# A spectral-layer kernel: its inverse stage in steps of two quarters, all products on 64x64 tiles

## The reference

```python
h = jnp.einsum('bhwi,ic->bhwc', x, fc0_w) + fc0_b          # 3 -> 64 channels
h = h.transpose(0, 3, 1, 2)
for l in range(LAYERS):                                     # 4
    sc = _spectral_conv(h, w1r[l] + 1j * w1i[l], w2r[l] + 1j * w2i[l])   # rfft2, 32x16 modes mixed, irfft2
    pw = jnp.einsum('bihw,oi->bohw', h, pw_w[l]) + pw_b[l][None, :, None, None]
    y = sc + pw
    mean = y.mean(axis=(0, 2, 3), keepdims=True)
    var = y.var(axis=(0, 2, 3), keepdims=True)
    y = (y - mean) * jax.lax.rsqrt(var + EPS)
    y = y * gamma[l][None, :, None, None] + beta[l][None, :, None, None]
    h = jax.nn.gelu(y, approximate=False)
```

## Time and profile before

| | us |
|---|---|
| median of 3 runs | 2692.91 (2688.74 to 2693.61) |
| profiled execution | 2692.11 |
| its span | 2690.3 |
| TensorE busy | 2267.7 (84%) |
| ScalarE busy | 1717.2 (64%) |
| VectorE busy | 1704.0 (63%) |
| bytes moved by DMA | 537.18 MB, mean 200 GB/s |

### The profile page before, as it was taken

One profiled execution on the slowest core, in us unless ns is written; L12 is line 12 of the kernel. 1 busy time (PEld: TensorE's weight loads), 2 busy tenths in 40 slices (PEclk: granted clock), 3 DMA queues, 4 the chain that ended last, 5 costly groups with the idle time before them and its releaser, 6 DMA issues. The chain is left out here.

```text
span 2690.3 us, 75014 instructions
## 1 busy us (share of the span) xinstructions
PE 2267.7 (84%) x32251; PEld 1466.2 (54%) x32251; DVE 1704.0 (63%) x2585; ACT 1717.2 (64%) x2771; POOL 191.9 (7%) x237
## 2 busy tenths in 40 slices
PE   7679989966997997699899859996993777765999
PEld 4556657754664776566567656662221666642444
DVE  4767878884776887577778757771005776634443
ACT  2823358875776887667678766777992777721333
POOL 0000000000000000000000000000002222202443
PEclk9889989998998999899999989998996899976999
DMA  5746577558997774799977379996541000012332
GB/s 173 237 144 219 213 275 258 192 191 277 360 347 281 279 248 153 247 350 361 335 266 259 124 249 328 366 341 233 179 140 35 1 1 1 1 26 63 88 87 60
DMA packets 179062, 537.18 MB, mean 200 GB/s; under 512 B 23183, under 2 KB 38223, under 8 KB 178511
## 3 DMA queue, kind: packets, MB, share of 16 engines
q1 hardware_dynamic: 178735, 532.38, 58.6%
HBM read 362.57 MB, written 170.37 MB: 198 GB/s over the span
## 5 line engine op out<-in xcount | busy, mean ns | idle before, releaser
L398 PE MATMUL P<-cst,mem 128*128 128x128 f32 (+1 forms) x3760 | 528.8, 284 | 54.2 <-ACT mem L661 13.9
L643 ACT ACTIVATE mem<-P,small 128x512 f32<-128x512 f32 x512 | 323.7, 684 | 365.0 <-PE P L505 279.6
L398 PEld LDWEIGHTS P<-cst,mem 128*128 128x128 f32 (+1 forms) x3760 | 412.1, 143 | 175.7 <-issue 123.0
L505 PEld LDWEIGHTS P<-cst,mem 64*128 64x128 f32 x4096 | 251.2, 188 | 212.8 <-DVE mem L774 107.1
L786 DVE BATCH_NORM_STATS2 mem<-mem 128x6 f32<-128x512 f32 x512 | 327.1, 681 | 42.4 <-ACT mem L643 41.4
L816 DVE COPY mem<-P 128x512 f32<-128x512 f32 x384 | 247.9, 686 | 100.4 <-PE P L398 99.1
L505 PE MATMUL P<-cst,mem 64*128 64x128 f32 x4096 | 301.1, 286 | 1.2 <-issue 1.1
L779 DVE COPY mem<-P 128x512 f32<-128x512 f32 x256 | 174.9, 686 | 144.7 <-PE P L486 144.7
L633 ACT ACTIVATE mem<-mem,small 128x1024 f32<-128x1024 f32 x192 | 237.9, 1239 | 37.4 <-DMA mem<-z_d 37.4
L774 DVE COPY mem<-P 128x512 f32<-128x512 f32 x256 | 176.7, 690 | 114.0 <-PE P L398 113.9
L661 ACT ACTIVATE mem<-mem,small 128x1024 f32<-128x1024 f32 x192 | 232.6, 1248 | 7.7 <-DMA mem<-z_d 6.7
(11 more groups left out here) (167 smaller groups left out, 3096.8 us busy)
## 6 DMA issues: line engine op xcount, KB each, us to landing
mem<-z_d SPq DMA_DIRECT2D x384, 512.0 KB, 5.3
z_d<-mem SPq DMA_DIRECT2D x256, 512.0 KB, 6.7
mem<-in_wmix SPq DMA_DIRECT2D x64, 1024.0 KB, 8.7
G_d<-mem SPq DMA_DIRECT2D x128, 256.0 KB, 4.0
mem<-G_d SPq DMA_DIRECT2D x128, 256.0 KB, 5.5
hz<-z_d SPq DMA_DIRECT2D x64, 512.0 KB, 4.6
mdB<-dT_d SPq DMA_DIRECT2D x44, 384.0 KB, 5.6
mem<-in_x SPq DMA_DIRECT2D x128, 12.0 KB
```

The lines of the kernel that those rows point to most:

```text
L398: return nc.tensor.matmul(out, in_, ident[0:n, 0:n], start=True, stop=True, is_transpose=True)
L505: last = nc.tensor.matmul(banks[x][:, j * 128:j * 128 + 128], ATs[o, a.q % 2, j * 128:j * 128 + 128], i2c[o, x * 128:x * 128 + 128], start ...
L643: nc.scalar.activation(ychunk(a, h), P[4 + 2 * (a.q % 2) + h][:, :], ACT.Identity, bias=bias0 if first else pwb_c).then_inc(S["eY"], 1)
```

## The change

Every engine's step is now taken for two quarters at once, at even q. TensorE does: transposes of both quarters (lag 4), the product over y of the quarter of the step itself (lag 0), the pointwise products of both, the products over x of both. The product over x is cut into 64x64 tiles: 16 products of 128 columns instead of 8. ScalarE does the GELU of two quarters (lag 2), then the results of two (lag 4); VectorE two transposed quarters (lag 4), two copies of the product over y (lag 0), the statistics of two (lag 6). SyncE still steps by quarters: it loads with lag -2 and stores with lag 6. In layer 0 it asks for the first two quarters ahead of the loop, as `mix_loads` does for the other layers. Buffers, semaphores and the conditions of the waits stay.

The diff; the old body of TensorE's step is left out, it stands above:

```diff
--- before.py
+++ after.py
@@ -321,22 +321,25 @@
                     for h in range(2):
                         sp.dma_start(Gt[n.par][:, h * 512:h * 512 + 512], G_s[n.t, n.par, h]).then_inc(gl[n.par], 16)
                 load_mixed(At(0, 0, 0, 0))
+                if first:
+                    for q in range(2):
+                        load_pixels(l, first, At(0, 0, q, 0))
 
                 def step(t, u, q):
-                    a = At(t, u, q, 0)
+                    a = At(t, u, q, -2)
                     n = At(t, u, q, -4)
                     if q == 0 and n.ok:
                         wait(sp, "pI1", l * 32 + n.pair * 2 - 2)
                         load_mixed(n)
-                    b = At(t, u, q, 8)
+                    b = At(t, u, q, 6)
                     if b.ok and b.q % 2 == 1:
 
                         sp.wait_ge(S["eY"], l * 128 + b.s * 2 + 2)
                         for x in range(2):
                             sp.dma_start(z_y[b.t, b.par, x, b.q // 2], ybuf[b.q // 2][:, x * 1024:x * 1024 + 1024]).then_inc(yst[b.q // 2], 16)
-                    if a.ok and (first or a.s >= 2):
+                    if a.ok:
                         if a.pair >= 2:
-                            sp.wait_ge(S["pY"], l * 128 + (a.pair - 2) * 8 + q // 2 * 4 + 4)
+                            sp.wait_ge(S["pY"], l * 128 + (a.pair - 2) * 8 + a.q // 2 * 4 + 4)
                         load_pixels(l, first, a)
                     if t == PAIRS // 2 and u == 0 and q < 2 and l + 1 < layers:
 
@@ -463,48 +466,62 @@
                     pe.wait_ge(S["eStat"], 1)
                 pw = wc6 if first else wbd
 
-                def step(t, u, q):
-                    a = At(t, u, q, 5)
-                    if a.ok:
-                        wait(pe, "eI1"
...
+                def transpose(a):
+                    wait(pe, "eI1", l * 64 + a.pair * 4 + 4)
+                    wait(pe, "eT3", l * 64 + a.s - 1)
+                    for i in range(4):
+                        j = 4 * a.q + i
+                        last = tr(P[2 + a.q % 2][:, i * 128:i * 128 + 128], Ai[a.par][:, j * 128:j * 128 + 128])
+                    last.then_inc(S["pT3"], 1)
+
+                def inverse_y(a):
+                    if a.q == 0:
+                        pe.wait_ge(gl[a.par], l * 256 + a.t * 32 + 32)
+                    wait(pe, "eI1", l * 64 + a.s)
+                    for m in range(8):
+                        for w in range(2):
+                            image, half = image_half(l, a.q // 2, w)
+                            for v in range(2):
+                                o, x, k = slice(v * 64, v * 64 + 64), image * 512 + m * 64, v * 128 + half * 64
+                                last = nc.tensor.matmul(P[v][w * 64:w * 64 + 64, m * 64:m * 64 + 64], Gt[a.par][o, x:x + 64], i1c[o, k:k + 64], start=True, stop=True)
+                    last.then_inc(S["pI1"], 1)
+
+                def pointwise(a):
+                    if first:
+                        pe.wait_ge(zl[a.par][a.q // 2 * 2], a.t * 32 + 32)
+                        pe.wait_ge(zl[a.par][a.q // 2 * 2 + 1], a.t * 32 + 32)
+                    else:
+                        pe.wait_ge(S["z_gelu_c"], (l - 1) * 64 + a.pair * 4 + a.q // 2 * 2 + 2)
+                    wait(pe, "eY", l * 128 + a.s * 2 - 2)
+                    for w in range(2):
+                        for x in range(2):
+                            o, n = slice(x * 64, x * 64 + 64), w * 2048 + a.q * 512
+                            nc.tensor.matmul(P[4 + 2 * (a.q % 2) + x][w * 64:w * 64 + 64, :], pw[o, o], zbuf[a.par][o, n:n + 512], start=True, stop=False)
+
+                def inverse_x(a):
+                    pe.wait_ge(S["eT3"], l * 64 + a.s + 1)
+                    for j in range(4):
                         for w in range(2):
                             for x in range(2):
-                                o, n = slice(x * 64, x * 64 + 64), w * 2048 + a.q * 512
-                                nc.tensor.matmul(banks[x][w * 64:w * 64 + 64, :], pw[o, o], zbuf[a.par][o, n:n + 512], start=True, stop=False)
-                        pe.wait_ge(S["eT3"], l * 64 + a.s + 1)
-                        for j in range(4):
-                            for x in range(2):
-                                o = slice(x * 64, x * 64 + 64)
-                                last = nc.tensor.matmul(banks[x][:, j * 128:j * 128 + 128], ATs[o, a.q % 2, j * 128:j * 128 + 128], i2c[o, x * 128:x * 128 + 128], start=False, stop=j == 3)
-                                if j == 3:
+                                o, c = slice(x * 64, x * 64 + 64), j * 128 + w * 64
+                                last = nc.tensor.matmul(P[4 + 2 * (a.q % 2) + x][w * 64:w * 64 + 64, j * 128:j * 128 + 128], ATs[o, a.q % 2, c:c + 64], i2c[o, x * 128:x * 128 + 128], start=False, stop=j == 3)
+                                if j == 3 and w == 1:
                                     last.then_inc(S["pY"], 1)
+
+                def step(t, u, q):
+
+                    if q % 2 == 0:
+                        a, b, n = At(t, u, q, 4), At(t, u, q + 1, 4), At(t, u, q, 0)
+                        if a.ok:
+                            transpose(a)
+                            transpose(b)
+                        if n.ok:
+                            inverse_y(n)
+                        if a.ok:
+                            pointwise(a)
+                            pointwise(b)
+                            inverse_x(a)
+                            inverse_x(b)
                 over_steps(pe, step)
 
                 pe.wait_ge(S["sAggr"], l + 1)
@@ -625,22 +642,30 @@
             def inv(l, first):
                 enter(act, "act", 2 * l + 2)
 
+                def pixels(c):
+                    z = zbuf[c.par][:, QCOL[c.q] * 1024:QCOL[c.q] * 1024 + 1024]
+                    wait(act, zl[c.par][c.q], 256 + (l - 1) * 128 + c.t * 16 + 16)
+                    nc.scalar.activation(z, z, ACT.Gelu, bias=bbi, scale=bsc).then_inc(S["z_gelu_c"], 1)
+
+                def result(a):
+                    for h in range(2):
+                        act.wait_ge(S["pY"], l * 128 + a.s * 2 + h + 1)
+                        if h == 0 and a.pair >= 1:
+
+                            if a.q % 2 == 0:
+                                act.wait_ge(yst[a.q // 2], (l * 16 + a.pair) * 32)
+                            act.wait_ge(S["eS"], l * 128 + a.s * 2 - 6)
+                        nc.scalar.activation(ychunk(a, h), P[4 + 2 * (a.q % 2) + h][:, :], ACT.Identity, bias=bias0 if first else pwb_c).then_inc(S["eY"], 1)
+
                 def step(t, u, q):
-                    c = At(t, u, q, 4)
-                    z = zbuf[c.par][:, QCOL[c.q] * 1024:QCOL[c.q] * 1024 + 1024]
-                    if c.ok and not first:
-                        wait(act, zl[c.par][c.q], 256 + (l - 1) * 128 + c.t * 16 + 16)
-                        nc.scalar.activation(z, z, ACT.Gelu, bias=bbi, scale=bsc).then_inc(S["z_gelu_c"], 1)
-                    a = At(t, u, q, 6)
-                    if a.ok:
-                        for h in range(2):
-                            act.wait_ge(S["pY"], l * 128 + a.s * 2 + h + 1)
-                            if h == 0 and a.pair >= 1:
-
-                                if a.q % 2 == 0:
-                                    act.wait_ge(yst[a.q // 2], (l * 16 + a.pair) * 32)
-                                act.wait_ge(S["eS"], l * 128 + a.s * 2 - 6)
-                            nc.scalar.activation(ychunk(a, h), P[4 + 2 * (a.q % 2) + h][:, :], ACT.Identity, bias=bias0 if first else pwb_c).then_inc(S["eY"], 1)
+                    if q % 2 == 0:
+                        a, c = At(t, u, q, 4), At(t, u, q, 2)
+                        if c.ok and not first:
+                            pixels(c)
+                            pixels(At(t, u, q + 1, 2))
+                        if a.ok:
+                            result(a)
+                            result(At(t, u, q + 1, 4))
                 if first:
                     act.wait_ge(S["eStat"], 1)
                 act.wait_ge(S["s_parload"], (l + 1) * 128)
@@ -766,24 +791,30 @@
                 if first:
                     nc.vector.tensor_tensor(bias0, P[6][:, 0:1], pwb_c, ALU.add).then_inc(S["eStat"], 1)
 
+                def transposed(a):
+                    dve.wait_ge(S["pT3"], l * 64 + a.s + 1)
+                    wait(dve, "pY", l * 128 + a.s * 2 - 2)
+                    nc.vector.tensor_copy(ATs[:, a.q % 2, :], P[2 + a.q % 2][:, :]).then_inc(S["eT3"], 1)
+
+                def inverse(a):
+                    v, b = a.q % 2, a.q // 2
+                    dve.wait_ge(S["pI1"], l * 32 + a.pair * 2 + b + 1)
+                    nc.vector.tensor_copy(Ai[a.par].rearrange("p (y h z k) -> p h y z k", h=2, z=2, k=2 * KX)[:, b, :, :, v * KX:v * KX + KX],
+                                          P[v][:, :].rearrange("p (k y z) -> p y z k", k=KX, z=2)).then_inc(S["eI1"], 1)
+
+                def moments(a):
```

(41 more changed lines are left out.)

1 line of the change is left out of this document (removed).

## The result

The change makes the kernel slower: 2759.8 us (median of 4, 2746.3 to 2772.1) against 2690.8, a ratio of 1.026 with a 95% interval of 1.0227 to 1.0292. The forecast was 2645 and faster. The profiled execution took 2772.1 us, its span is 2770.3, 80 more than before.

The account below looks back on a forecast made before the run. TensorE was taken to bound layer 0's inverse stage, TensorE and DMA nearly at once those of layers 1 to 3. Layer 0's -18 and the others' -29 gave -47 us, from 2692 to 2645; range 2608 to 2680.

Parts of the forecast that it names:

- Layer 0: Inverse stage of layer 0: TensorE's two-quarter step falls from 6.33 to 5.77 us, saving 18 us (11 to 24).
- Steady: Running steps of layers 1 to 3: DMA limits them to 6.46 us, 0.11 less in 28 steps, -3 us a layer.
- Nothing is sooner: Pixel loads in layers 1 to 3: counted by finished quarters, they are asked for no sooner than before; no gain.
- Fill and end: Start and finish of the stages in layers 1 to 3: -3 us and -4 us a layer, the end -3 in layer 3.
- Rival C: TensorE, waiting in lumps for DMA in layers 1 to 3, loses its clock: slower, 2729 us; chance 0.06.
- Rival B: DMA is the bound outright, layers 1 to 3 give nothing, only layer 0's 18 us: 2674 us; chance 0.16.
- Rival A: DMA engines have room, steps of layers 1 to 3 come to 6.0 us: 2602 us; chance 0.14.
- Rival D: The 64x64 products over x do not overlap, step 7.8 us: about 2837 us; chance 0.02.

Follow-up runs that it names:

- experiment 2: The kernel before the change, old order kept, with only the product over x cut into 64x64 tiles: 2771.1 us, ratio 1.032.
- the hybrid: The changed kernel with 64x64 tiles for the product over x in layer 0 alone, 64x128 in layers 1 to 3: 2636.9 us, ratio 0.981.
- experiment 9: 64x64 tiles in layer 0 alone, as in the hybrid, with only 256 of 1024 columns of each store stored in layers 1 to 3: 2581.9 us.

## Why the prediction was wrong

- **Layer 0: right, and a little too careful.** The working gave 5.77 (1.01, 0.98, 1.76, 0.93 + 1.09); measured 5.58 undisturbed (1.02, 0.98, 1.72, 1.86) and 5.69 on the mean. Even here three blocks stop TensorE for 0.3 to 0.4 each; that is 1.1 of the 3 us by which 28 steps exceed 5.58, the rest I did not account for. Gain over the 28 steps 18, with fill and end 21; forecast 18. TensorE waited for neither VectorE nor ScalarE there, as worked out. The two parts overlap: order alone brings 6.33 to 5.82, tiles alone to 5.95, which would be 0.89 together and is 0.64. The Trainium skill, TensorEngine Tiling (Array Packing), Key Properties, has a change of tiling mode drain the engine. The trace fits: with the new tiles in the old order, the change between pointwise product and product over x is gone, and the second begins 0.86 after the first, not 0.97 as in the earlier trace rows. That is 0.11 of the 0.19 a quarter which these tiles save; how much of it is the narrower weight load was not separated. From experiment 2:

```profile
704.61 1.04 PE L500 MATMUL P<-mem,wbd 64*64 64x512 f32 x8
705.47 1.05 PE L506 MATMUL P<-cst,mem 64*64 64x128 f32 x32
```

- **Layers 1 to 3, "Steady": the step that failed.** It said: TensorE's own 5.77 is below what DMA allows, so 6.46. It knew two bounds, work and bytes, and put the third, the supply of TensorE's instructions, at nothing without a reason. Measured 7.96 to 8.06: +115 us where -9 stood. The runs show the third bound: 240 records 6.4 to 6.7 whatever the order, 304 records 7.4 to 8.1 whatever the order and the requests, 336 records 8.5 to 8.7, that is, for the two larger numbers, 6.2 to 6.8 us per block of 256; and 304 records 5.8 to 5.9 once the loads are small.
- **"Nothing is sooner" of the pixel requests** stands: the waits of SyncE bear it out, and no run shows otherwise. What the prediction did not weigh is that the time of the request matters at all: asked for up to two quarters later than before or after, the pixels take 0.4 to 0.7 off a step of 304 records and add 0.14 to 0.20 to one of 240.
- **Fill and end**: -3 and -4 a layer forecast, -8.8, -4.5 and -2.2 together measured. Right in sign, in all -15.5 against -20; layer 3, without prefetch, gave a third of its 6, and layer 0's own -3.3 stood at nothing (0.9 - 0.7).
- **Rival C** (2729) had the nearest time and the wrong cause: there TensorE was to wait in lumps for pixels and lose its clock. It does stop in lumps, but for its instructions, and the clock falls as a consequence (0.91 to 0.92 in the three stages, 0.96 to 0.97 before). After the stop of 3.24 us in

```profile
707.79 0.66 PE L507 MATMUL P<-cst,mem 64*64 64x128 f32 x13 [3.24 <-issue]
...
709.96 1.99 PE L486 MATMUL P<-cst,mem 64*64 64x64 f32 x64
```

the product over y takes 1.99 instead of 1.16; the granted clock is 0.94 of full from 660 to 800, where it was 1.00. By that, an estimate, 12% of the time ran at 1.2 GHz, half speed, and some 8 us were lost; idle time is 28.7.
- **Rival B** (bytes alone bound) falls for the change; the hybrid comes near it at 6.4 to 6.5, with blocks still in part its bound (experiment 9). **Rival A** falls: the version with the old tiles, whose own step is 5.82, got 370 GB/s at a share of 1.02 and steps of 6.4, not 6.0. The Trainium skill, DMA: Bandwidth & Descriptors, has about 425 for a core alone and 358 where HBM binds; the run's 370 lies between, nearer the second.
- **Rival D** falls: 64 records of the product over x, 32 to a quarter, take 1.93, where tiles one after the other would have taken 1.94 for a quarter alone.

Shown: that the loss follows the number of TensorE's records in the presence of the pixel loads, and goes with either; and, block by block, that each stop ends with the landing of the next block. A block lands about one block ahead of its use at the most: even in layer 0 of the kernel before, where TensorE never stops, it lands 3.1 to 7.0 us before it, with blocks 6.6 apart. Open: when a block is asked for, and why full loads delay the start of its packet more than stores do.

## What to carry to other kernels

Count an engine's instructions as a third resource beside its work and its bytes: here 256 TensorE instructions took 6.2 to 6.8 us beside large loads, so 38 to 41 a microsecond is the most that such a stage sustained. An "issue" gap inside a run of products that wait for nothing was that bound showing; a cut into smaller tiles, which doubles the records of that product, then belongs only in stages without large loads. And a change made of two parts is to be timed as two: the order alone gained 1.7%, the tiles alone lost 3.2%, and the order everywhere with the tiles in layer 0 alone gains 1.9%.

## What the runs showed that I had not expected

- Loads and stores are not alike for the blocks: at DMA shares of 0.68 with loads a step of 304 records takes 6.3 to 6.55, at 0.76 with stores 5.81 to 5.87.
- Bytes reached 370 GB/s over 140 us at a share of 1.02, where the kernel before reached 354 at 1.01; a share of 0.93 in the changed kernel went with 291. The share alone does not tell how much room is left.
